# Products of probabilities with values sent for two units at a time in the softmax half of a mixer kernel

## What is computed

```python
def _L0_attn_b_ref(x, Wq, bq, Wk, bk, Wv, bv, Wo, bo):
    q = (x @ Wq + bq).reshape(Bb, Ss, H, HD)          # H = 16 heads of HD = 16
    k = (x @ Wk + bk).reshape(Bb, Ss, H, HD)
    v = (x @ Wv + bv).reshape(Bb, Ss, H, HD)
    scores = jnp.einsum('bthd,bshd->bhts', q, k) / jnp.sqrt(HD)
    scores = jnp.where(causal, -jnp.inf, scores + alibi)
    attn = jax.nn.softmax(scores, axis=-1)
    out = jnp.einsum('bhts,bshd->bthd', attn, v).reshape(Bb, Ss, Dd)
    return out @ Wo + bo
```

## Time and profile before

| | us |
|---|---|
| median of three runs | 2462.08 |
| lowest and highest | 2460.75, 2468.25 |
| the profiled execution | 2463.02 |
| its span, first to last instruction | 2461.2 |
| PE, DVE, ACT busy in it | 2114.0, 1690.0, 1261.7 |
| softmax half: first to last exponential begins at | 1091.8, 2335.5 |
| a full batch of it (the fifth) | 159.20 |

### The profile page before, as it was taken

One profiled execution on the slowest core, in us unless ns is written; L12 is line 12 of the kernel. 1 busy time (PEld: TensorE's weight loads), 2 busy tenths in 40 slices (PEclk: granted clock), 3 DMA queues, 4 the chain that ended last, 5 costly groups with the idle time before them and its releaser, 6 DMA issues.

```text
span 2461.2 us, 58530 instructions
## 1 busy us (share of the span) xinstructions
PE 2114.0 (86%) x24838; PEld 1206.1 (49%) x24838; DVE 1690.0 (69%) x3750; ACT 1261.7 (51%) x2049; POOL 735.8 (30%) x665
## 2 busy tenths in 40 slices
PE   3667988989898998388799999999999999988963
PEld 2445665666665664234355454544544545544432
DVE  5666666565665635478788787887887887777227
ACT  2324243434425222127676766667667676666713
POOL 1131323323232101342354243361533513212110
PEclk9789999999999999669999999999999999999987
DMA  3201111111101102243234142331332312313063
GB/s 101 69 19 53 36 36 52 35 36 36 47 24 36 36 18 86 86 113 112 73 88 127 41 122 65 87 121 37 113 96 70 113 36 67 91 27 131 1 239 137
DMA packets 131540, 179.28 MB, mean 73 GB/s; under 512 B 9120, under 2 KB 95136, under 8 KB 131280
## 3 DMA queue, kind: packets, MB, share of 16 engines
q1 hardware_dynamic: 129104, 175.02, 23.2%
q10 hardware_dynamic: 2176, 0.52, 0.1%
HBM read 97.40 MB, written 77.59 MB: 71 GB/s over the span
## 4 chain that ended last, share of the span: by engine, by line
PE 64%; DVE 23%; ACT 6%; issue 4%; POOL 1%; DMA 1%; SPq 0%; DVEq 0%; POOLq 0%; ACTq 0%
PE general L929 12%; PE out_of_heads L800 9%; PE general L612 8%; DVE maxima L1496 8%; PE scores L755 6%; PE general L598 4%; PE general L940 4%; PE general L586 3%; PE turned_scores L769 3%; PE general L578 3%; PE scores L644 2%; PE out_of_heads L686 2%; DVE ln L1478 2%; DVE probs_turned L1439 2%; PE out_of_heads L696 2%
## 5 line engine op out<-in xcount | busy, mean ns | idle before, releaser
L1496 DVE TENSOR_REDUCE maxima<-scores 128x1 f32<-128x512 f32 (+3 forms) x1536 | 795.9, 553 | 228.8 <-PE scores L731 117.0
L1135 ACT ACTIVATE probs_turned<-turned_scores 128x512 f32<-128x512 f32 x1152 | 679.9, 601 | 354.0 <-PE turned_scores L731 181.1
L755 PE MATMUL scores<-k_stacks,q_stacks 59*128 59x512 bf16 (+3 forms) x1536 | 444.4, 335 | 59.9 <-DVE maxima L1496 54.4
L769 PE MATMUL turned_scores<-q_stacks,k_stacks 61*128 61x512 bf16 (+3 forms) x1536 | 436.1, 329 | 9.4 <-ACT probs_turned L1135 9.4
L755 PEld LDWEIGHTS scores<-k_stacks,q_stacks 59*128 59x128 bf16 x1536 | 124.0, 94 | 286.9 <-DVE maxima L1496 219.4
L1837 POOL TENSOR_TENSOR ln_low<-ln 128x512 bf16<-128x512 f32 x128 | 139.1, 1094 | 292.8 <-DVE ln L1478 292.7
L1816 POOL TENSOR_SCALAR ln<-x_for_attention,ln_mean_var,ln_rstd 128x256 f32<-128x256 f32 x104 | 134.1, 1298 | 207.7 <-DVEq L1650 111.1
L1055 ACT ACTIVATE gate_tanhs<-general,feature_vectors 128x512 f32<-128x512 f32 x96 | 66.0, 688 | 224.7 <-PE general L612 177.3
L800 PE MATMUL out_of_heads<-probs_turned,values_odd_and_heads_out 128*17 128x512 f32 (+3 forms) x1536 | 153.8, 496 | 1.3 <-ACT probs_turned L1135 1.3
L800 PE MATMUL out_of_heads<-probs_turned,values 128*17 128x512 f32 (+3 forms) x1536 | 153.5, 495 | 0.0
L769 PEld LDWEIGHTS turned_scores<-q_stacks,k_stacks 61*128 61x128 bf16 x1536 | 125.5, 94 | 51.2 <-ACT probs_turned L1135 18.5
(11 more groups left out here) (257 smaller groups left out, 5265.8 us busy)
## 6 DMA issues: line engine op xcount, KB each, us to landing
x_after_attention<-x_residual SPq DMA_DIRECT2D x16, 1024.0 KB, 5.0
x_times_wo<-x_wo_out SPq DMA_DIRECT2D x64, 256.0 KB, 2.2
q_stacks<-q_stack SPq DMA_DIRECT2D x64, 256.0 KB, 4.5
k_stacks<-k_stack SPq DMA_DIRECT2D x64, 256.0 KB, 4.8
x_for_attention<-in_x SPq DMA_DIRECT2D x8, 1024.0 KB, 5.5
x_residual<-in_x SPq DMA_DIRECT2D x8, 1024.0 KB, 5.4
x_for_attention<-x_after_attention SPq DMA_DIRECT2D x8, 1024.0 KB, 5.5
ffn_h<-x_times_wo SPq DMA_DIRECT2D x32, 256.0 KB, 5.9
```

Source lines behind the costliest of these rows:

```text
L755: mx = pe.matmul(bank_s[:, first * P:(first + tiles) * P], QS[at_s:at_s + QROWS, r, i * P:(i + 1) * P], KS[at_s:at_s + QROWS, r, k0 * P:(k ...
L769: ex = pe.matmul(bank_t[:, first * P:(first + tiles) * P], KS[at_t:at_t + KROWS, r, j * P:(j + 1) * P], QS[at_t:at_t + KROWS, r, i0 * P:(i ...
L1135: nc.scalar.activation(PR[:, s % SLOTS, :], TB[s % 2][:, :], ACT.Exp).then_inc(sem["ex_taken"], 1)
L1496: r = dve.tensor_reduce(MP[:, gg % 2, g, at:at + 1], max_bank[m][:, first * P:(first + tiles) * P], AX.X, ALU.max)
```

## The change

The products with values of a group's units were sent one unit at a time, at steps 7, 11, 15, ... 35 of the group and step 3 of the next: always behind the scores of a unit's last step, one unit late. Now a table names the steps: units 0 and 1 at step 10 of the group, 2 and 3 at 18, 4 and 5 at 26, 6 and 7 at 34, and unit 8 at step 3 of the next group, as before. The number of products and all other calls stay.

```diff
+VALUES_AT = {10: (0, 1), 18: (2, 3), 26: (4, 5), 34: (6, 7), 3: (8,)}
...
                 attend(s, b, k)
-                if kk % HEADS == HEADS - 1 and 0 < s // HEADS <= STEPS // HEADS:
-                    values_unit(s // HEADS - 1)
+                for u in VALUES_AT.get(kk, ()):
+                    unit = NU * (gg if kk > HEADS else gg - 1) + u
+                    if 0 <= unit < NU * GROUPS * B:
+                        values_unit(unit)
                 if kk == 27 and group_in(gg + 1):
                     turn_max(gg + 1)
```

## The result

| | before | after |
|---|---|---|
| median, us | 2462.16 | 2510.78 |
| lowest, highest | 2460.75, 2468.25 | 2510.21, 2513.9 |
| ratio, 95% interval | | 1.0195 (1.0176 to 1.0214) |
| span of the profiled execution | 2461.2 | 2509.5 |
| first to last exponential of the softmax half begins at | 1091.8, 2335.5 | 1091.3, 2385.0 |

What follows compares the result with a forecast made beforehand. PE was taken to set the pace almost everywhere in the softmax half. The terms sum to 6.75 us per full batch, 40.5 for six, plus 3 in the last and 0 in the first: +43, 2505 us, range about 2480 to 2530.

Steps and rivals of the forecast that it cites:

- b: Behind the transpose of maxima, scores wait until DVE has read the previous ones: 0.63, four times, 2.5 us per batch.
- c: Fills (projections and gates between scores) wait at eight places for banks ACT or DVE must empty: 4.7 us per batch.
- a: TensorE's changes of work around the products with values fall from 21 to 16 a group: 2.0 us saved per batch.
- d: Near steps 34 and 35, where DVE sets the pace, its maxima start later behind the double burst: 0.65 us.
- e: Gate operations on DVE at steps 91 and 127 start later: 0.4 each, 0.8 us for both.
- f: Behind each double burst two sets of scores follow closely and PE waits at the third: 0.5 us per batch.
- g: Waits that go, on ACT at step 47 and a little at step 20: 0.4 us saved.
- The first rival: Fewer changes of work win, the waits being hidden: 16 us less, 2446; chance 0.05.
- that nothing remains: Rival: no net change, savings and partly hidden waits leaving some 1 us per batch, 2462 to 2470; chance 0.04.
- Starved DVE: Rival: DVE runs out of scores at every double burst, some 75 us more, 2537; chance 0.09.

Runs made afterwards that it cites:

- the burst put back: The changed kernel with units 4 and 5 merged at step 27 instead of 26: 2498.27 us, 1.0141 of the kernel before.
- the pair that covers little: The kernel before with only units 2 and 3 merged, at step 19 instead of 18: 2462.79 us, ratio 0.9994.
- the four pairs: Four kernels, each the kernel before with one pair merged (0, 1; 2, 3; 4, 5; 6, 7): 2467.57, 2466.03, 2487.85, 2480.02 us.

## Why the prediction was right, and where its terms were off

It forecast 2505 and slower; it is 2510.8. A full batch was to take 166, and takes 166.9. The mechanism was right: work that stood in the shadow of the single bursts is laid bare, at the places named in b and c. That the sum came so close is in part luck: places that were not foreseen cost 1.6, and 0.9 instead of 0.4 of waits went. Per full batch, term by term:

| term | forecast | measured | from |
|---|---|---|---|
| a, changes of work | -2.0 | -2.0, taken over | double burst 1.85, lone one 0.99 |
| b, transpose of maxima | +2.5 | +2.3 | units 4, 5 alone; 2.1 with the burst put back, 2.2 with unit 5 alone moved |
| c, banks of the fills | +4.7 | +4.8 | eight places, below |
| d, stretch that DVE sets | +0.65 | +0.9 | units 6, 7 alone, first group |
| e, gate operations | +0.8 | +0.8 | units 2, 3 alone, last two groups |
| f, close scores | +0.5 | +0.2 | what is left in units 0, 1 and 6, 7 alone |
| g, waits that go | -0.4 | -0.9 | steps 20, 47, 92 to 95 |
| not forecast | | +1.6 | three places, below |
| sum | 6.75 | 7.7 | the batch itself: 7.7 |

That the sum closes is no test of each row: a is the forecast's own price, and f and the last row are in part what the others leave over. Counted step by step in the changed kernel alone, 16 double bursts at 1.94 in place of 20 single ones at 1.08 and 12 at 0.98 give -2.3 for a; b is 2.2, g is -1.0, and the places not forecast cost 1.8.

**a.** 1.85 was the forecast for a double burst and is the measurement. The changes of work are saved and then lost again. By the Trainium skill, TensorEngine Tiling (Array Packing), "Key Properties", a change of tiling mode drains TensorE. The runs agree but show how little that decides: the pair that covers little won 0.5 per batch. The first rival's case called the waits of b, c and d three times this gain; at 7.85 against 2.0 they are nearly four times.

**b.** The wait was forecast at 0.63 and is 0.61, four times. Its worth was too large by one group: in the first one DVE is late a few steps on, so that PE gets little for being sooner. A wait ahead of a stretch that another engine sets is no term of its own.

**c.** From the scores to the first fill product an undisturbed step takes 0.22 (0.34 with masks). After, the excess is 0.43 at step 8 (1740.81 to 1741.46), 0.37 at 16, 0.51 at 24, 0.25 at 60, 0.81 at 68, 0.45 at 80, 0.84 at 116; at step 104 it is some 1.1 (steps 100 to 108 are 0.9 longer with units 6 and 7 alone, and two changes cheaper). Forecast were 0.34, 0.5, 0.42, 0.5, 0.75, 0.5, 0.76 and 0.98. The five places that were worked out each came 0.06 to 0.12 too small (3.7 against 3.25), the three taken at 0.5 too large (1.07 against 1.5); that the sums agree within 0.1 is luck. Working back from when the bank is free, place by place, was the step that carried the forecast. Its mechanism was incomplete at step 104, where a bank of scores is late first. The idle figure in brackets understates these waits (0.26 at step 8, where start to start says 0.43):

```profile
1740.81 0.39 PE L756 MATMUL scores<-k_stacks,q_stacks 59*128 59x512 bf16 x1
...
1741.46 0.39 PE L930 MATMUL general<-ln_turned_high,w_high 64*128 64x512 bf16 x2 [0.26 <-ACT qk_block L1168]
```

By the Trainium skill, Perfetto Trace Analysis, "Tensor Engine Instruction (MATMUL, LD_WEIGHTS)", the end of a matmul is computed, not observed; starts were the safer measure here.

**d, e, f.** The first group with only units 6 and 7 merged is 0.73 longer, less two changes of work saved: 0.93. The last two groups with only units 2 and 3 merged give 0.0 and +0.37; with the 0.2 that each saves, 0.8 is the cost. Term f is hardly there: the third scores behind a double burst mostly come late enough. Term g was too small by the wait that the merge of units 0 and 1 takes out of steps 92 to 95.

**Not forecast.** A third wait on maxima at step 96, where the kernel before had two, at steps 94 (the 0.24 of the earlier trace rows) and 95. Steps 94 to 96 after:

```profile
1840.32 0.39 PE L756 MATMUL scores<-k_stacks,q_stacks 59*128 59x512 bf16 x1 [0.30 <-DVE maxima L1499]
...
1841.64 0.39 PE L756 MATMUL scores<-k_stacks,q_stacks 59*128 59x512 bf16 x1 [0.29 <-DVE maxima L1499]
...
1842.93 0.37 PE L756 MATMUL scores<-k_stacks,q_stacks 59*128 59x512 bf16 x1 [0.31 <-DVE maxima L1499]
```

The burst at step 23 of the group had covered it; with the like at step 132 it is 0.5 (what units 4 and 5 alone cost in the last two groups, less the transpose's 0.67 each). At steps 72 to 76, where DVE has two-piece maxima and a norm's chain, PE loses 0.45 in pieces of 0.1. Steps 48 to 59 lose 0.7 (0.3 with units 0 and 1 alone, 0.4 with 2 and 3); in the changed kernel only 0.15 of it lies at the transposes of steps 56 and 58, the rest in small pieces at steps 49 to 53. All three are places where a burst had stood shortly before and the prediction did not look.

**The other batches.** The first cost nothing, as forecast: 138.6 against 135.7, but with two short stretches at the lower clock that the kernel before does not have there, 1.4 each (the fourth batch before against the fifth). The last was sized low: 3 was a guess without rows, and it is 4.7 (from its turn to its last exponential 153.4 against 148.7, two such stretches in each). The second of them in the changed kernel stands at its very end and falls on a double burst, which takes 3.26 to the next scores instead of 1.85:

```profile
2380.97 3.32 PE L801 MATMUL out_of_heads<-probs_turned,values_odd_and_heads_out 128*17 128x512 f32 x16
2384.23 0.60 PE L770 MATMUL turned_scores<-q_stacks,k_stacks 61*128 61x384 bf16 x2
```

```profile
2381.30:2384.70 3.40, 3.40 (x19) 0.68 (x12) 0.27 (x1) 2.20 (x2) 1.12 (x1) 0.50 0.00 0
```

At equal clock, five full batches at 7.7, the sixth at 8.1, 4.7 and nothing for the first make 51.3; one low stretch fewer in all (five against six) gives back 1.4: 49.9, against 50.0 for the softmax half.

**The rivals.** That the changes of work win fell with the four pairs; that nothing remains fell with the batches. Starved DVE (2537) was half seen: DVE idles 2.34 behind a double burst, but pairs at the old steps cost only 2.5 per batch, and banks less saved changes account for that.

## What to carry to other kernels

Before work is moved or merged on the engine that sets the pace, list what waits end in its shadow: every bank that another engine must empty while it runs, and every ring with two places whose next reader stands behind it. Take each shadow away on paper and work out when the resource is free; these sums, from start times, were right to some 0.1 us at the places where they were worked out, and the saving of a merge was a fifth of what the shadows were worth. And look at all places where the work stood, not only those where a known buffer changes hands.

## What the runs showed of the hardware

The granted clock falls to its lower level (0.50, 1.2 of 2.4 GHz) for short stretches in the middle of dense work, 2 to 9 of them in the softmax half of one execution. One in the kernel before, and one after:

```profile
1548.70:1552.10 3.40, 3.11 (x27) 2.21 (x31) 1.90 (x6) 2.63 (x5) 2.49 (x1) 0.50 0.28 54
```

```profile
1398.30:1401.70 3.40, 3.27 (x31) 2.29 (x35) 1.91 (x5) 2.63 (x5) 2.33 (x1) 0.50 0.69 145
```

Both come just behind the turn of a batch, where PE had stood still for 1.17 us (0.99 in the second); another stop, of 0.45, spans the start of the stretch. Not every turn has one, and not every one stands at a turn: in the changed kernel two fall into the first batch (1159.4 and 1179.8). Which batches have them differs from kernel to kernel, so a comparison of batches has to be made at equal clock, and differences of a few us between medians are not the edit's alone.
